# Sort-based sparsemax attention: turned scores as products of row strips instead of turned copies of the kept scores

## The reference, cut to what matters

```python
queries = (query @ Wq + bq).reshape(B, L, 16, 8)
keys = (key_param @ Wk + bk).reshape(B, 32, 16, 8)
z = einsum('blhe,bshe->bhls', queries, keys) / sqrt(8)
z_sorted = -sort(-z);  cum = cumsum(z_sorted)
k_sup = sum(1 + k * z_sorted > cum)
tau = (cum[k_sup - 1] - 1) / k_sup
A = maximum(z - tau, 0)                     # then A @ values, @ Wo + bo
```

## Time and profile before

| | |
|---|---|
| median of three runs | 3134.96 us |
| profiled execution | 3136.26 us, span 3134.5 us |
| TensorE busy in the span | 2599.7 us (83%) |
| VectorE busy | 1995.2 us (64%) |
| ScalarE busy | 1468.9 us (47%) |
| the function of the change | from 2580 us to the end of the span |
| mean granted TensorE clock in the span | 0.887 of 2.4 GHz |

### The profile page before, as it was taken

The page is one execution under the profiler, slowest core; times in us unless marked ns, Lnnn a source line. Parts: engine busy times, 40 slices in busy tenths (PEclk is TensorE's granted clock), DMA queues, the critical chain, the costliest instruction groups (busy, mean ns, idle before and its releaser), DMA issues. The chain is left out here.

```text
span 3134.5 us, 53684 instructions
## 1 busy us (share of the span) xinstructions
PE 2599.7 (83%) x20884; PEld 1494.5 (48%) x20884; DVE 1995.2 (64%) x3935; ACT 1468.9 (47%) x3051; POOL 582.5 (19%) x565
## 2 busy tenths in 40 slices
PE   6888889999599799979978998689979984657655
PEld 3555546666344344435544444455654642434433
DVE  7988745565587455557754543678872247887882
ACT  6676557777232132213334443278842323545543
POOL 1344311111000133324420000011113040000000
PEclk9999889999799899979988998789979995777766
DMA  1000010000000000010000000110011110000000
GB/s 61 2 2 2 2 40 4 8 8 1 4 1 0 32 2 2 1 43 12 12 5 1 0 1 19 43 54 9 8 54 43 39 54 4 11 21 21 14 17 7
DMA packets 41994, 51.98 MB, mean 17 GB/s; under 512 B 9291, under 2 KB 30868, under 8 KB 40724
## 3 DMA queue, kind: packets, MB, share of 16 engines
q1 hardware_dynamic: 39700, 44.39, 4.5%
q0 software_dynamic: 2048, 4.20, 0.5%
HBM read 39.39 MB, written 9.18 MB: 15 GB/s over the span
## 5 line engine op out<-in xcount | busy, mean ns | idle before, releaser
L130 POOL TENSOR_TENSOR l_rstd<-l_moments,const_minus_half 128x4 f32<-128x4 f32 x96 | 105.9, 1103 | 1401.9 <-DVE l_moments L124 1396.9
L1426 PE MATMUL l_p_gate<-l_h_t,w_wg 128*128 128x512 f32 x400 | 208.8, 604 | 0.0
L1449 PE MATMUL l_p_out<-l_hidden,w_wd 128*128 128x512 f32 x400 | 204.4, 594 | 2.6 <-DVE l_hidden L1719 2.5
L804 DVE TENSOR_REDUCE l_top<-l_ring 128x8 f32<-128x1024 f32 x128 | 150.9, 1221 | 79.4 <-PE l_ring L638 79.3
L2991 DVE SCALAR_TENSOR_TENSOR l_mix<-l_decay,l_cb 128x1024 f32<-128x1024 f32 x128 | 172.3, 1358 | 36.9 <-ACT l_decay L2869 35.9
L2869 ACT ACTIVATE l_decay<-l_p_ring 128x1024 f32<-128x1024 f32 x128 | 130.0, 1023 | 97.9 <-PE l_p_ring L2743 96.5
L350 ACT ACTIVATE l_probs<-l_probs,l_minus_top 128x128 f32<-128x128 f32 x512 | 156.8, 393 | 33.6 <-DVE l_minus_top L410 33.5
L1719 DVE TENSOR_TENSOR l_hidden<-l_act_out,l_p_spread 128x512 f32<-128x512 f32 x128 | 85.7, 685 | 128.6 <-ACT l_act_out L1547 128.3
L1209 DVE TENSOR_REDUCE l_minus_top<-l_p_score 128x4 f32<-128x1024 f32 x64 | 78.2, 1224 | 106.1 <-PE l_p_score L1037 102.5
L3647 DVE TENSOR_TENSOR l_srt<-l_srt 128x1024 f32<-128x1024 f32 (+3 forms) x112 | 115.7, 1033 | 27.0 <-ACT l_srt L3513 24.5
L753 ACT ACTIVATE l_probs_t<-l_ring 128x1024 f32<-128x1024 f32 x64 | 62.0, 1022 | 149.2 <-PE l_ring L662 149.2
(11 more groups left out here) (503 smaller groups left out, 6347.7 us busy)
## 6 DMA issues: line engine op xcount, KB each, us to landing
l_c_t<-in_ctx_t SPq DMA_DIRECT2D x24, 256.0 KB, 2.7
l_rows_in<-l_zero SPq DMA_DIRECT2D x1, 2432.0 KB
l_tile_h<-l_rows_in SPq DMA_DIRECT2D x38, 64.0 KB, 1.9
l_rows_out<-l_tile_y SPq DMA_DIRECT2D x38, 64.0 KB, 1.5
w_mask<-in_mask SPq DMA_DIRECT2D x1, 2048.0 KB, 9.2
w_wg<-in_l2f_wg SPq DMA_DIRECT2D x1, 2048.0 KB
w_wu<-in_l2f_wu SPq DMA_DIRECT2D x1, 2048.0 KB
w_wd<-in_l2f_wd SPq DMA_DIRECT2D x1, 2048.0 KB
```

Of the source, the lines that this page charges most:

```text
L130: return nc.gpsimd.tensor_tensor(rstd[:, :], moments[:, :, 1], minus_half[:, 0:moments.shape[1]], ALU.pow)
L804: nc.vector.tensor_reduce(top[:, b % 2, half * HALF:(half + 1) * HALF, 0], s, AX.X, ALU.max)\
L1426: nc.tensor.matmul(p_gate[k % 2][:, :], w["wg"][:, s, :], h_t[:, g % 4, :], start=True, stop=True)\
L1449: nc.tensor.matmul(p_out[:, :], w["wd"][:, s, :], hidden[:, k % 4, :], start=(s == 0), stop=(gated and s == steps - 1)).then_inc(down, 1)
```

## The change

The turned scores are no longer turned copies of `z`. They are computed again, as products of `keys` and `q_t` with the operands swapped: (head, key) by tokens. The four heads of bank `b` have their channels in rows 32 b to 32 b + 31, so each bank is one product over a strip of 32 rows, and the four banks use the four strips of the array. The threshold is added the same way: `minus_tau` is laid out so that turning it puts the four heads of bank `b` in rows 32 b to 32 b + 3, the other rows being zero, and `spread` has a block for each strip. All eight products of a group stand together at BEHIND + 1, the first four starting the banks, the second four ending them. `clip_turned` of banks 0 and 1 stands at BEHIND + 2, of 2 and 3 at BEHIND + 3. `z` needs one buffer, `q_t` gets two.

```diff
-        q_t = L.sbuf("q_t", [D, GROUP * T])
+        q_t = L.sbuf("q_t", [D, 2, GROUP * T])
-        z = L.sbuf("z", [T, 2, ROWS, S])
+        z = L.sbuf("z", [T, ROWS, S])
-        minus_tau = L.sbuf("minus_tau", [T, 2, ROWS])
-        tau_t = L.sbuf("tau_t", [HEADS, GROUP * T])
-        spread = L.sbuf("spread", [HEADS, HEADS, S])
+        minus_tau = L.sbuf("minus_tau", [T, GROUP, 4, S])
+        tau_t = L.sbuf("tau_t", [T, GROUP * T])
+        spread = L.sbuf("spread", [T, 4, S])
...
+                strip = lambda b: slice(32 * b, 32 * b + 32)
...
-                        last = nc.tensor.transpose(p_out[0:HEADS, u, :], minus_tau[:, k % 2, u * HEADS:(u + 1) * HEADS], const["ident"][:, :])
+                        last = nc.tensor.transpose(p_out[:, u, :], minus_tau[:, u, :, :], const["ident"][:, :])
...
-                def transposes(k, b):
+                def turned_scores(k):
                     pe.wait_ge(tau_t_ready, k + 1)
                     pe.wait_ge(z_ready, GROUP * min(k + 2, NG))
-                    nc.tensor.matmul(p_s[b][:, :], spread[:, 4 * b:4 * b + 4, :], tau_t[:, :], start=True, stop=False)
-                    for u in range(GROUP):
-                        row = u * HEADS + 4 * b
-                        last = nc.tensor.matmul(p_s[b][:, u * T:(u + 1) * T], z[:, k % 2, row:row + 4, :], const["ident"][:, :],
-                                                start=False, stop=(u == GROUP - 1))
-                    last.then_inc(turned, 1)
+                    for b in range(4):
+                        nc.tensor.matmul(p_s[b][:, :], keys[strip(b), 4 * b:4 * b + 4, :], q_t[strip(b), k % 2, :],
+                                         start=True, stop=False)
+                    for b in range(4):
+                        nc.tensor.matmul(p_s[b][:, :], spread[strip(b), :, :], tau_t[strip(b), :], start=False, stop=True)\
+                            .then_inc(turned, 1)
...
+                    if (k := group_at(g, BEHIND + 1)) is not None:
+                        turned_scores(k)
                     for b in range(4):
-                        if (k := group_at(g, BEHIND + 1 + b)) is not None:
-                            transposes(k, b)
                         if (k := group_at(g, BEHIND + 3 + b)) is not None:
                             weigh(k, b)
...
-                    nc.scalar.copy(tau_t[:, :], p_out[0:HEADS, :, :]).then_inc(tau_t_ready, 1)
+                    nc.scalar.copy(tau_t[:, :], p_out[:, :, :]).then_inc(tau_t_ready, 1)
...
-                        if (k := group_at(g, BEHIND + 2 + b)) is not None:
+                        if (k := group_at(g, BEHIND + 2 + b // 2)) is not None:
                             clip_turned(k, b)
...
-                    nc.vector.tensor_copy(spread[:, :, :], bcast(const["ident"][0:HEADS, 0:HEADS], [HEADS, HEADS, S], 2))
+                    nc.vector.memset(minus_tau[:, :, :, :].rearrange("p u b i -> p (u b i)"), 0.0)
+                    for b in range(4):
+                        rows = slice(32 * b, 32 * b + 32)
+                        nc.vector.tensor_copy(spread[rows, :, :], bcast(const["ident"][rows, 32 * b:32 * b + 4], [32, 4, S], 2))
...
-                    nc.vector.tensor_reduce(minus_tau[:, k % 2, :], ranked, AX.X, ALU.max, negate=True).then_inc(tau_ready, 1)
+                    nc.vector.tensor_reduce(minus_tau[:, :, :, 0:4].rearrange("p u b i -> p (u b) i"),
+                                            ranked.rearrange("p (n i) e -> p n i e", i=4), AX.X, ALU.max, negate=True).then_inc(tau_ready, 1)
```

More of the change, by code:

```diff
@@ L3259, in step_buffers @@
         def step_buffers(k, n):
-            return (srt[(n - 1) % 2][:, :, :] if n else z[:, k % 2, :, :]), srt[n % 2][:, :, :]
+            return (srt[(n - 1) % 2][:, :, :] if n else z[:, :, :]), srt[n % 2][:, :, :]
         def pairs(t, p, k):
@@ L3324, in scores @@
                     for u in range(GROUP):
-                        nc.tensor.matmul(p_s[u][:, :], q_t[:, u * T:(u + 1) * T], keys[:, :, :], start=True, stop=True)\
+                        nc.tensor.matmul(p_s[u][:, :], q_t[:, k % 2, u * T:(u + 1) * T], keys[:, :, :], start=True, stop=True)\
                             .then_inc(scored, 1)
@@ L3498, in copy_queries @@
                     act.wait_ge(proj, k + 1)
-                    nc.scalar.activation(q_t[:, :], p_hq[:, :], ACT.Identity, bias=scaled_bq[:, 0:1], scale=scale)\
+                    nc.scalar.activation(q_t[:, k % 2, :], p_hq[:, :], ACT.Identity, bias=scaled_bq[:, 0:1], scale=scale)\
                         .then_inc(q_ready, 1)
@@ L3503, in copy_scores @@
                     act.wait_ge(scored, GROUP * k + u + 1)
-                    nc.scalar.copy(z[:, k % 2, u * HEADS:(u + 1) * HEADS, :], p_s[u][:, :]).then_inc(z_ready, 1)
+                    nc.scalar.copy(z[:, u * HEADS:(u + 1) * HEADS, :], p_s[u][:, :]).then_inc(z_ready, 1)
                 def keep_ends(k, n):
```

## The result

The changed kernel takes 3090.63 us (median of four runs, 3089.46 to 3092.05), the kernel before 3135.19 beside it: ratio 0.9855 [0.9841, 0.9869]. That is 44.6 us less, where 37.5 were forecast (3097.5 us). The profiled execution has a span of 3088.9 us, 45.6 under that of before.

The account below looks back on a forecast made before the run. VectorE, the fuller engine, was taken to bound the kernel, with only its waits to gain: 29.9 - 3.6 + 8.5 + 3.5 - 1.0 = 37.3 us, so a forecast median of 3097.5 us, range 3084 to 3122.

Parts of the forecast that it names:

- What bounds the periods: Six like periods: VectorE is the fuller engine, idle 57.4 us, so the change can give back only its waits.
- The strips: Turned scores on TensorE: all four banks cost 3.85 us at the half clock, 2.0 at the full; cross_transposes stay at +6.7.
- Rival C: Strips don't run side by side: 16 instructions take 15.5 us, the kernel is slower at about 3181 us; chance 3%.
- The switch of the array's shape: TensorE between strips and products of another shape: no drain shown in the trace, switches fall from eight to two, nothing taken.
- Half clock until about +12: Walk through a period: TensorE at half clock until about +12 us after the threshold's end, full after it.
- Rival A: Clock is up by cross_values: step 5 doesn't wait, cross_add at +15.95, 49.2 us gained, 3086 us; chance 17%.
- The 29.9: Six like periods: waits at cross_add and the sort shrink, gaining 4.98 us per period, 29.9 us for six.
- The slower projection, -3.6: Behind cross_add: the clock may be down, so two more periods pay for a 6.76 us projection, 3.6 us lost.
- The first period: Period from 2643.3 to 2696.9, without cross-attention: 8.5 us gained, 7.2 if the projection takes 6.76 us rather than 5.48.
- The tail, 3.5: After the last sort: projection starts at +19.55, 5.1 us earlier, but is charged 5.48 us instead of 3.85; 3.5 net.
- Set-up and what was taken at nothing: Set-up's memset and four copies lose 1.0 us; z and q_t buffers, the strided threshold and wider turn_tau cost nothing.

Follow-up runs that it names:

- e3_pairs_per_strip: The changed kernel with each bank's keys and spread products one after the other, instead of four and four: 3089.38 us, ratio 0.985.
- e4_clip_per_step: The changed kernel with ScalarE's four clips one per step, as before, instead of two and two: 3096.62 us, ratio 0.9876.
- e5_turns_full_rows: The kernel before with only each bank's spread product over 128 rows instead of 16, turning products kept: 3143.99 us against 3171.14, ratio 0.991.
- e2_full_rows: The changed kernel with each bank's two products in the old place, one bank a step, and over all 128 rows: 3107.38 us, ratio 0.9905.
- e1_bank_by_bank: The changed kernel with each bank's two 32-row products in the old place, one bank a step, no strips side by side: 3156.98 us, ratio 1.0057.
- e6_first_set_twice: The changed kernel with the first four strip products (keys) issued twice: 3137.73 us against 3171.14 for the kernel before, ratio 0.9895.

## Why the prediction was right, and where its terms were off

- **What bounds the periods: right.** The gain is VectorE's waits, 33.9 of 34.0 us, with its work untouched.
- **The strips: right.** 16 instructions in 3.73 us at the half clock (3.85 from the earlier trace rows), `cross_transposes` at +6.7. TensorE's busy time in the function fell by 60 us (12.1, 39.5 and 8.5 by the windows), not by 8 x 9 = 72. Rival C (the strips in line) did not occur.
- **The switch of the array's shape: nothing to see.** Between the strips and `cross_transposes` there is no gap in the timeline above. The Trainium skill, TensorEngine Tiling (Array Packing), Key Properties, speaks of a drain at a change of mode; the trace shows none as idle time, though a drain hidden in the modelled end of a product would not show there.
- **"Half clock until about +12": a step that failed, though cheaply.** In the profiled trace `cross_values` took 1.16 us at +8.5, not 1.92 to +10.55, and sort step 5 doesn't wait at all (0.85 forecast). Rival A had this. But A's full clock to the end failed too: it dips before `cross_add`, which comes at +16.5 (forecast 16.85, A 15.95). In the sum: waits at `cross_add` 13.5 us (10.8 forecast), at the sort 0 (5.1). The 29.9 should have been 32.3. Where the forecast's clock did come, in two periods of `e3_pairs_per_strip`, its walk holds closely (waits 0.81 and 1.54 us for 0.85 and 1.8, `cross_add` at +16.6 for +16.85).
- **The slower projection, -3.6: wrong, and the largest miss.** I let two more periods pay for a projection of 6.76 us. It takes 5.44 to 5.48 us in all six, also the one that had 6.76 before, and the waits for it fell from 5.0 us to 3.4: +1.6, so 5.2 us off. Together the six periods gave 34.0, not 26.3; A had 35.1. The slow projection does exist with these products: `e3_pairs_per_strip` and `e4_clip_per_step` each have one in six periods (6.61 and 6.68 us, with waits of 2.18 and 2.26 us).
- **The first period: right,** 7.4 us of 8.5, at the price named for a slow projection (7.2), and it was slow (6.46 us): its sort waits are gone and `add_output` waits 2.1. The 8.5 holds a slip: 9.7 less 0.6 and 0.4 is 8.7.
- **The tail, 3.5: undersized,** 7.1 us. In the timeline of the tail the projection starts 17.2 us after the last threshold's end (19.55 forecast, A 18.1) and took the 3.85 us of the full clock, where I charged 5.48:

```profile
3031.84 1.88 PE L3348 MATMUL l_p_s<-l_a_t,l_vals_of 128*128 128x512 f32 x4
3034.85 3.85 PE L3355 MATMUL l_p_s<-l_o_of,w_wo 32*128 32x128 f32 x128 [1.12 <-ACT l_o_of L3485]
```

- **Set-up and what was taken at nothing: right.** 0.7 us (1.0 forecast). The threshold with its strided output is unchanged, and the memset of `minus_tau` (485 ns) and the four copies into `spread` (202 ns each) cost what their nearest rows said:

```profile
L3672 DVE TENSOR_REDUCE l_minus_tau<-l_srt 128x64 f32<-128x2048 f32 x8 | 18.3, 2286 | 0.3
```

The errors nearly all point one way, too little gain, so nothing cancelled. The time lies inside the stated range, but nearer to rival A (3086 us, 4.6 away) than to the forecast (3097.5, 6.9 away). The path, the waits and the price of the strips were right; the clock behind +7, in the periods and in the tail, was taken too low.

The Trainium skill, TensorE: Matmul & The Clock Gate, Why this matters for your kernels, says that unbroken work brings the full clock. The runs here narrow that. The run of 32-row products had TensorE busy without a break at 0.50 from +7 to +12, the run of 128-row products at 1.00 with the same instructions. The argument against A in the prediction (19.9 us busy at 0.50 in the earlier trace rows) was a true reading with the wrong scope: it came from products of 16 rows among others of 128, and the change replaces exactly those. The prediction noted for A that "the strips fill all rows" and then gave it 17%. Nor is A a rule: the same strips had a late clock in one or two of six periods in five of the traces above.

## What to carry to other kernels

A product over few rows cost more than its own time here: TensorE, busy with them among others, sat at half clock for longer, and padding the operands with zero rows gave 27 us (`e5_turns_full_rows` against before) and 50 us (`e2_full_rows` against `e1_bank_by_bank`) for no less work. Read the granted clock in short pieces of several like periods, not as one mean: the mean fell from 0.72 to 0.71 while every period got shorter, and like periods of one trace can take two courses. One trace may show only one of them, so look at those of near variants too, and ask what each course costs: about 2 us or more at `cross_add` in the kernel before, under 0.5 with the products of the change. After a change has shortened the path to a waiting instruction, look again at how many instructions stand in front of it: one line then gave 9.5 us more.

## What was not expected of the hardware

- Rows against the clock: 0.65 over six periods and 372.4 us with one 32-row strip at a time, 0.73 and 339.9 us with 128 rows. With four strips side by side the clock was up by +8.5 in all six periods of both traces of the change, but in only four of six in `e3_pairs_per_strip` and in the three traces of the change with a later `cross_add`.
- Four strips of a float32 product of 512 columns take as long as one: 3.73 us for eight products in four strips at the half clock, where one bank's two products alone took 3.71 (2890.22 to 2893.93). TensorE's timeline of that run, `e1_bank_by_bank`:

```profile
2890.22 2.07 PE L3339 MATMUL l_p_s<-l_q_t,l_keys 32*128 32x512 f32 x2 [1.83 <-ACT l_tau_t L3475]
2892.09 1.91 PE L3341 MATMUL l_p_s<-l_tau_t,l_spread 32*128 32x512 f32 x2
2893.93 1.11 PE L3383 MATMUL l_p_cross<-const_ident,l_probs 128*128 128x128 f32 x4
```

- The clock fell before `cross_add` in the change, from +12 on, where TensorE was busy 3.93 of 5.00 us, and not in the two runs where it was busy for all of that stretch with 128-row products. Idle pieces alone don't explain it: in `e6_first_set_twice` the clock stays at 1.00 from +12 to +17 in all six periods with TensorE busy 3.7 to 4.1 of 5.00 us. The cause stays open.
